# Two transformer layers on one core: weight casts moved to ScalarE, one mask loaded earlier, the first k's residuals made on VectorE

## The reference

```python
# pass 0 (layer 0): self-attention under a key mask, a gate from the context, then the MLP
n = layer_norm(x, g1, be1)
x = x + self_attn(n, mask) + (ctx @ Wg.T + bg)        # q, k, v = n @ W.T + b
x = x + relu(layer_norm(x, g2, be2) @ W1.T + b1) @ W2.T + b2
# pass 1 (layer 1): causal self-attention
x = mha(layer_norm(x), layer_norm(x), causal=True) + x
# pass 2 (layer 1): attention over the context, then the MLP
y = mha(layer_norm(x), ctx, causal=False) + x
out = y + relu(layer_norm(y) @ w1 + b1) @ w2 + b2
```

## Time and profile before

| | us |
|---|---|
| median of 3 runs (1502.21 to 1504.9) | 1502.92 |
| the profiled execution: its time | 1503.33 |
| its span in the profile | 1501.5 |
| TensorE busy | 1393.0 (93%) |
| VectorE busy | 1144.6 (76%) |
| ScalarE busy | 1037.7 (69%) |
| GpSimd busy | 833.8 (56%) |

### The profile page before, as it was taken

The page is one execution under the profiler, slowest core; times in us unless marked ns, Lnnn a source line. Parts: engine busy times, 40 slices in busy tenths (PEclk is TensorE's granted clock), DMA queues, the critical chain, the costliest instruction groups (busy, mean ns, idle before and its releaser), DMA issues.

```text
span 1501.5 us, 39428 instructions
## 1 busy us (share of the span) xinstructions
PE 1393.0 (93%) x13620; PEld 1163.5 (77%) x13620; DVE 1144.6 (76%) x3860; ACT 1037.7 (69%) x2104; POOL 833.8 (56%) x1139
## 2 busy tenths in 40 slices
PE   6889999999999999998888888889999999999998
PEld 5579989998899888876766666657777877777867
DVE  3888888888888888777787778677677777777763
ACT  4777777777777776566766767566767667767655
POOL 4455555555555565755565545455666655666632
PEclk8999999999999999999999999999999999999999
DMA  6554443433444333444654565554334434334400
GB/s 181 149 152 125 133 114 114 114 113 115 125 128 114 114 114 106 148 120 136 185 148 139 159 170 138 152 148 138 103 114 130 128 103 119 101 117 128 109 18 27
DMA packets 161589, 187.09 MB, mean 125 GB/s; under 512 B 15984, under 2 KB 136176, under 8 KB 161392
## 3 DMA queue, kind: packets, MB, share of 16 engines
q1 hardware_dynamic: 161104, 183.78, 42.6%
q10 hardware_dynamic: 288, 0.79, 0.2%
HBM read 125.78 MB, written 58.72 MB: 123 GB/s over the span
## 4 chain that ended last, share of the span: by engine, by line
PE 71%; ACT 9%; issue 7%; DVE 6%; POOL 5%; DMA 1%; SPq 1%; DVEq 0%; POOLq 0%; ACTq 0%
PE d_ps L518 27%; PE d_ps L820 10%; PE o_ps L667 10%; PE s_ps L590 8%; PE t_ps L604 7%; PE t_ps L637 5%; ACT q_stack L882 3%; PE m_ps L525 2%; DVE prob L1052 2%; ACT prob_t L874 2%; POOL ot_lo L1295 1%; PE t_ps L641 1%; ACT h_f L982 1%; ACT tf_a L891 1%; DVE o_q L1140 1%
## 5 line engine op out<-in xcount | busy, mean ns | idle before, releaser
L874 ACT ACTIVATE prob_t<-t_ps 128x384 f32<-128x384 f32 (+1 forms) x512 | 275.7, 549 | 254.7 <-PE t_ps L637 148.9
L590 PE MATMUL s_ps<-k_stack,q_stack 96*128 96x256 bf16 (+1 forms) x1536 | 284.2, 266 | 19.9 <-DVE top L1052 8.3
L865 ACT ACTIVATE prob<-prob,neg_max 128x256 f32<-128x256 f32 x512 | 230.8, 505 | 66.2 <-DVE neg_max L1052 63.3
L1295 POOL TENSOR_TENSOR h_lo<-h_f,h_hi 128x512 fp32r<-128x512 f32 x124 | 159.4, 1286 | 112.6 <-DVE h_hi L1184 102.5
L1052 DVE CUSTOM_DVE_ANT_0 prob<-s_ps,bias_sb 128x256 f32<-128x256 f32 x512 | 194.5, 417 | 28.4 <-PE s_ps L590 26.4
L637 PE MATMUL t_ps<-q_stack,k_stack 108*128 108x256 bf16 (+1 forms) x1024 | 201.2, 263 | 16.1 <-ACT q_stack L882 15.8
L1037 DVE TENSOR_REDUCE top<-s_ps 128x2 f32<-128x512 f32 x256 | 170.4, 681 | 50.0 <-PE s_ps L590 48.5
L590 PEld LDWEIGHTS s_ps<-k_stack,q_stack 96*128 96x128 bf16 x1536 | 116.0, 98 | 108.2 <-issue 51.2
L667 PE MATMUL o_ps<-prob_t,v_sb 128*17 128x256 f32 (+1 forms) x3072 | 191.2, 367 | 0.0
L1052 DVE CUSTOM_DVE_ANT_0 prob<-s_ps,causal 128x128 f32<-128x128 f32 (+1 forms) x512 | 157.1, 352 | 36.5 <-PE s_ps L590 35.5
L604 PE MATMUL t_ps<-ident_sb,prob 128*128 128x128 f32 x1024 | 155.5, 274 | 1.5 <-DVE prob_t L1250 1.5
(11 more groups left out here) (156 smaller groups left out, 4001.9 us busy)
## 6 DMA issues: line engine op xcount, KB each, us to landing
parts<-q_part SPq DMA_DIRECT2D x96, 192.0 KB, 2.3
parts<-k_part SPq DMA_DIRECT2D x96, 192.0 KB, 2.3
q_stack<-parts SPq DMA_DIRECT2D x96, 192.0 KB, 3.3
k_stack<-parts SPq DMA_DIRECT2D x94, 192.0 KB, 3.3
q_stack<-parts SPq DMA_DIRECT2D x96, 128.0 KB, 3.1
k_stack<-parts SPq DMA_DIRECT2D x94, 128.0 KB, 3.2
ct_kept<-ct_hl SPq DMA_DIRECT2D x16, 512.0 KB, 3.9
x_in<-x_mid SPq DMA_DIRECT2D x32, 256.0 KB, 3.3
```

What stands on the lines that cost most here:

```text
L590: last = mm(s_ps[:, h % 2, q * S:q * S + n], q_stack[0:ROWS, t.par, head_of(t, h), q * P:(q + 1) * P], k_stack[0:ROWS, t.par, head_of(t, h ...
L865: last = nc.scalar.activation(prob[:, h % 4, q, :], prob[:, h % 4, q, :], ACT.Exp, bias=neg_max[:, h % 4, q:q + 1], scale=-1.0)
L874: nc.scalar.activation(prob_t[:, h % 8, 0:n], t_ps[:, h % 2, 0:n], ACT.Exp, scale=-1.0)\
L1295: g.tensor_tensor(dst, a, b, ALU.subtract).then_inc(done, 1)
```

## The change

Three edits, all below in full. First, the 24 casts of units 1 to 8 are made by ScalarE (`UNIT_ON_ACT`), in the same slots as before; the casts of unit 0 stay on VectorE, and so does every subtraction on GpSimd. In a slot the cast stands ahead of the copy of turned probabilities and of the exponentials in pass 0, and behind ScalarE's exponential in passes 1 and 2. Second, the mask of task 1 is loaded at slot 1 of step -1 in place of slot 0 of step 0. Third, in step -1 alone both subtractions of k move from GpSimd to VectorE, and the addition that takes v out of PSUM (`values_out`) moves from slot 5 to slot 8, behind them.

```diff
+UNIT_ON_ACT = (1, 2, 3, 4, 5, 6, 7, 8)
...
-                if h == 0 and has(st.nxt, (0,)):
+                if h == 0 and has(st.nxt, (0,)) and st.s:
                     if st.prev:
                         sp.wait_ge(u_done.sem, u_done.after(st.prev))
                         sp.sem_inc(passed, 1)
...
                     sp.dma_start(x_in[:, st.nxt2.par], tokens(source(st.nxt2))).then_inc(x_landed.of(st.nxt2), 16)
+                if h == 1 and st.s == -1:
+                    sp.dma_start(bias_sb[:, st.nxt2.par], tokens(mask[st.nxt2.b])).then_inc(mask_landed.of(st.nxt2), 16)
                 if h == 2 and has(st.prev):
...
                     affine((tf_a,) if st.nxt2.p == 0 else (xt_hi, tf_a), c, c + 2, xt_f)
+                if (st.s, h) in UNIT_AT and UNIT_AT[st.s, h][0] in UNIT_ON_ACT:
+                    u, n = UNIT_AT[st.s, h]
+                    if n == 0:
+                        act.wait_ge(unit_landed, 16 * (u + 1))
+                        unit_users_done(act, u)
+                    place, hi, _ = piece_io(u, n)
+                    nc.scalar.activation(hi, place, ACT.Copy).then_inc(unit_hi, 1)
                 t, ht = head_at(st, h, LAG, (0,))
...
-                if has(st.nxt, FIRST) and h == V_AT[0] + 1:
+                if has(st.nxt, FIRST) and h == (8 if st.s == -1 else V_AT[0] + 1):
                     values_out(st)
                 if h == st.split_at[1] and has(st.nxt):
+                    if st.s == -1:
+                        dve.wait_ge(k_p1.sem, k_p1.after(st.nxt))
+                        v.tensor_tensor(k_f[:, :, :], k_f[:, :, :], k_part[:, 0], ALU.subtract).then_inc(k_r.sem, 1)
                     dve.wait_ge(k_r.sem, k_r.after(st.nxt))
                     v.tensor_copy(k_part[:, 1], k_f[:, :, :]).then_inc(k_p2.sem, 1)
+                    if st.s == -1:
+                        dve.wait_ge(k_p2.sem, k_p2.after(st.nxt))
+                        v.tensor_tensor(k_part[:, 2], k_f[:, :, :], k_part[:, 1], ALU.subtract).then_inc(k_p3.sem, 1)
...
-                if (st.s, h) in UNIT_AT:
+                if (st.s, h) in UNIT_AT and UNIT_AT[st.s, h][0] not in UNIT_ON_ACT:
                     u, n = UNIT_AT[st.s, h]
...
-                if h == st.qk_at[1] + 2 and has(st.nxt):
+                if h == st.qk_at[1] + 2 and has(st.nxt) and st.s != -1:
...
-                if h == st.split_at[1] and has(st.nxt):
+                if h == st.split_at[1] and has(st.nxt) and st.s != -1:
                     pool.wait_ge(k_p2.sem, k_p2.after(st.nxt))
                     sub(k_part[:, 2], k_f[:, :, :], k_part[:, 1], k_p3.sem)
```

## The result

| | before | changed |
|---|---|---|
| median of 5 runs each, us | 1502.92 | 1494.47 |
| the profiled execution: time, us | 1503.33 | 1495.08 |
| its span, us | 1501.5 | 1493.2 |
| mean granted clock of that execution | 0.992 | 0.994 |

The ratio is 0.9933, with an interval of 0.9919 to 0.9948; a second measurement of the same file gave 0.9935 (0.9922 to 0.9949). So the change takes off 9.8 to 10 us by ratio and 8.3 by the profiled pair. The forecast was 6.8: the direction was right and the gain was under-sized. One execution of a later run, e16_before_filled31, took 2238.32 us at a mean clock of 0.557 and enters no figure here.

The account below looks back on a forecast made before the run. The prediction took TensorE to bound the kernel, busy 35.00 of 35.00 us in the steady part of pass 0. Its terms summed to -6.8 us from the profiled 1503.33, giving 1496.3 us, with an 80% range of 1493.2 to 1500.4.

Parts of the forecast that it names:

- First k's residuals: Step -1: GpSimd holds VectorE's first subtraction, the layer norm of task 1 starts later, and first scores follow; +0.5 us.
- The mask: Step 0: VectorE's 3.66 us wait for the mask of task 1 goes, only partly on the path; -2.2 us.
- Unit 1: Step 0: VectorE is relieved of four casts, three of them in the chain at 0.34 us; -0.8 us.
- The clock: After the mask in step 0: TensorE idles less, so the 3 us at 0.51 clock may shorten; -0.4 us.
- Unit 2: Step 1: casts leave the chain that ends in TensorE's 3.83 us wait for the output projection's operand; -1.2 us.
- Unit 3: Step 14: casts leave the stretch from x_in to x_hat, for which TensorE waits; -1.1 us, ends -0.4 and -1.2.
- Units 5 and 6: Steps 18 to 25: each step loses its cast on VectorE, which falls into a ScalarE gap of 0.56 us; -1.2 us.
- Unit 7: Step 30: TensorE's 2.76 us wait for GpSimd's third w_lo shortens to near 2.2; -0.5 us.
- ScalarE's price: Each cast takes ScalarE 0.60 us, of which 0.48 delays what is behind it.
- ScalarE takes the gain back: Rival: 24 casts on ScalarE each pass 0.2 us on to TensorE, +4.8 us, giving 1501.1 us; chance 7%.
- slower: Rival: ScalarE bounds wherever a cast stands, each delaying TensorE by 0.48 us; 1512.7 us, deciding from 0.4 a cast; chance 3%.
- more than the sum: Rival: GpSimd does not hold the subtraction, the clock stays full and unit 2 gives 1.9 us; 1493.5 us; chance 14%.

Follow-up runs that it names:

- e16_before_filled31: Kernel before, with 64 small TensorE products ahead of step 1's first output projection and 44 ahead of step 31's first projection; ratio 0.9998.
- e1: Kernel before, with only the mask of task 1 loaded at slot 1 of step -1; ratio 0.9984.
- e2: Kernel before, with only the 24 casts of units 1 to 8 moved to ScalarE; ratio 0.9960.
- e5: Changed kernel without the edit of the first k: casts and mask alone; ratio to the kernel before 0.9944.
- e14: Kernel before, with 64 small TensorE products ahead of step 1's first output projection and 44 ahead of step 30's first projection; ratio 1.0013.
- e3: Kernel before, with only the moves of the first k's residuals and of v in step -1; ratio 0.9985.
- e9: Changed kernel measured once more, unchanged; ratio to the kernel before 0.9935.
- e4: Changed kernel, with v of task 0 taken out at slot 5 again; ratio to the kernel before 0.9930.
- e11: Changed kernel, with v at slot 5 and 32 small products in place of 40 in step -1; ratio to the kernel before 0.9943.
- e13: Changed kernel, with 34 small TensorE products ahead of step 1's first output projection and 36 ahead of step 30's first projection; ratio to the kernel before 0.9947.
- e17: Changed kernel, with only 34 small TensorE products ahead of the first output projection in step 1; ratio to the kernel before 0.9958.
- e7: Changed kernel, with unit 3's third cast (step 14, slot 14) back on VectorE; 9.33 us from x_in to the end of x_hat.
- e6: Changed kernel, with each of the 24 casts on ScalarE done twice; ratio to the kernel before 0.9982.
- e8: Changed kernel, with unit 3's first two casts (step 14, slots 12 and 13) back on VectorE; 10.83 us from x_in to the end of x_hat.
- e18: Changed kernel, with v of task 0 at slot 5 and the second rounding of q and k of steps 0 and 1 on ScalarE; ratio to the kernel before 0.9934.
- e12: Changed kernel, with the second rounding of q and k of steps 0 and 1 on ScalarE; ratio to the kernel before 0.9941.

## Why the prediction fell short

- **First k's residuals, +0.5: wrong in sign.** The hold of VectorE and the later x_in came as forecast. The step "x_in, the turn, the 40 products and the first scores all follow x_in" failed. The end of the 40 products goes with the clock, and k_stack's arrival is the other bound: without this edit and with an early clock TensorE waits 1.0 to 1.6 us for it (e1, e2, e5, e14, e16), and the earlier k parts then count. In the one pair of profiles with equal starts it is worth -0.5 (e5 against the changed kernel); by itself it gave a ratio below 1 (e3, 0.9975 to 0.9995), part of which may have come through the mask. Its size is not settled better than that.
- **The mask, -2.2: right**, 2.3 to 2.4 against the profile before; against e3's, where the mask landed earlier, it would be 1.2. **Unit 1, -0.8: right**, 10.70 - 9.91, and 9.90 or 9.91 in all ten profiles with its casts on ScalarE, the mask early, full clock there and the roundings left on VectorE.
- **The clock, -0.4: mis-sized.** This term is the larger part of the miss: at that place it was 1.0, and over the whole program some 3.0. I priced one stretch, and the execution before has five, the start included. How the clock would fall elsewhere I did not ask.
- **Unit 2, -1.2**: right. The profiled pair shows 0.8, but e9 took 78.17 - 50.53 = 27.64 us from the turn to the projection, against 28.91 before, 1.3 less; e4, e11, e13 and e17 took 27.64 to 27.68, and e1, e14 and e16 28.91 to 28.93. Why the changed kernel's first profile took 28.14 is open.
- **Unit 3, -1.1 with an end of -1.2: mis-sized by a factor of two, shown** by e7. I read the earlier trace rows to the start of x_hat and took 1.22. What TensorE waits for is its end, and its length, 1.68 against 0.73 one row above, stood in the same rows. The missing 0.95 is GpSimd's hold, which the cast itself timed.
- **Units 5 and 6, -1.2**: 1.0. A step went from 21.91 to 21.78, forecast 21.75. In that profile the steps from 26 to 30 took 21.79 each, 0.05 more than before; in e9 it is 21.76, so that is no effect of the change. **Unit 7, -0.5: right**; TensorE's wait is 2.27, forecast near 2.2. **Units 4 and 8, +0.1: right** to within 0.2.
- **ScalarE's price**, 0.60: 0.62. The rival in which ScalarE takes the gain back shows only where the casts are doubled (e6), and there in steps 0, 1 and 14 and not in pass 1. The threshold in the rival *slower* was miscounted: 24 x 0.4 is 9.6 and not 9.8.

Without the clock the sum was -6.4, and at equal clock 6.9 to 7.3 were measured. That looks closer than it is: with unit 3 at -2.17 and k at -0.5 the sum would be -8.5, and some 1.2 to 1.6 us of it are not found in the time. The rival "more than the sum" named the clock and unit 2, but one of its reasons was that GpSimd does not hold VectorE, and it does. The Trainium skill, SBUF — State Buffer, section Who interferes with whom, has the later instruction wait for the whole of the earlier; the rows of e7, e8 and step -1 agree, and e8 adds that a second GpSimd instruction can go ahead of the waiting engine's next one.

What stays open is the last 3 us. That the mean clock is higher in the changed kernel is measured; that shorter waits cause it is only argued. Filled waits raised the mean clock of the kernel before and not that of the changed kernel, and no filling made its kernel faster by more than the noise. The line through the executions of one kernel is a correlation, too: it says what goes with a lower clock, and not what one would gain by raising it.

## What to carry to other kernels

Read the length of an instruction at the head of a chain as well as its start: an unusual length beside a GpSimd instruction is a wait, and what you move may be what timed it. When a wait is hidden behind another one, price both: here the clock's rise hid k_stack, and the edit that looked like a loss was a gain in the one profile pair that can tell. And when two kernels differ by less than 1%, compare executions at the same mean clock as well before explaining the difference.

## What the runs showed of the hardware

- On average a stretch of half clock goes with less than the work lost in it: 0.001 of mean clock is 1.5 us of full-speed time in a program of 1500 us, and the executions of the kernel before differ by 1.04. The place decides: 3 us at half clock cost 1.5 us in step 30 (25.55 against 24.08), 1.0 near 44 (11.70 against 10.69), and nothing that shows near 48 in e1 (10.71, against 10.70 in e3) or near 46 in e18 (10.90, as in e12 at full clock).
- The stretches come at different places in executions of one and the same program. The profiles hold 10.4 (e9) to 30.7 us (e6) at half clock in all, the start included. The five with filled waits hold 20.5 to 24.2, the kernel before 23.9 and the changed kernel 17.1 in its first profile.
- GpSimd and VectorE pass the memory between them instruction by instruction: x_hat took 0.73, 1.69 or 2.62 us as GpSimd's subtraction started 0.10 behind its end, 0.16 behind its start, or 0.07 ahead of it. ScalarE's copies from SBUF to SBUF took 0.61 to 0.63 us on average in every group, the 48 of e6 too, with GpSimd at work beside them.
